# Reordering the LayerNorm and expert loop of a transformer layer on eight cores

## What is computed

```python
x = _layernorm(x + attention(x, wq, wk, wv, wo))      # 16 heads of 128, softmax over 4096 keys
# the expert part, for each row n of x:
logits = x_flat @ Wr.T + br                           # 8 experts
probs = softmax(logits)
expert_idx, expert_weight = argmax(probs), max(probs)
h = einsum('nd,erd->ner', x_flat, A)                  # rank 64 for each expert: 512 columns
y = einsum('ner,eor->neo', h, B) * (1 / 64)
out = y[expert_idx] * expert_weight
x = _layernorm(x + out)
```

## Time and profile before

| | us |
|---|---|
| three timed runs | 4432.73, 4554.11 (the median), 4914.57 |
| profiled execution, device time | 4425.88 |
| its span, slowest core (0) | 4424.3 |
| spans of the eight cores | 4404.7 to 4424.3 |
| mean granted TensorE clock of the cores | 0.880 to 0.884 |

### The profile page before, as it was taken

One profiled execution on the slowest core, in us unless ns is written; L12 is line 12 of the kernel. 1 busy time (PEld: TensorE's weight loads), 2 busy tenths in 40 slices (PEclk: granted clock), 3 DMA queues, 4 the chain that ended last, 5 costly groups with the idle time before them and its releaser, 6 DMA issues.

```text
span 4424.3 us, 52274 instructions; the slowest of 8 cores (4404.7 to 4424.3 us)
## 1 busy us (share of the span) xinstructions
PE 3912.7 (88%) x15488; PEld 1369.4 (31%) x15488; DVE 2271.8 (51%) x4046; ACT 1388.4 (31%) x1574; POOL 187.0 (4%) x303
## 2 busy tenths in 40 slices
PE   6999999999799999999999999999999997835551
PEld 2444444444222222222222222222222233312220
DVE  0000000000388878788878888878887721253443
ACT  1111111111034444444444444444444520201110
POOL 0000000000000000000000000000000000000000
PEclk9999999999778989898989888989998988957776
DMA  9444943393200000000000000000000305120003
GB/s 139 77 76 77 158 77 77 77 146 71 67 1 25 6 20 25 25 1 25 25 25 1 25 25 25 2 24 25 25 1 25 52 6 76 20 38 1 1 1 152
DMA packets 196283, 192.34 MB, mean 43 GB/s; under 512 B 79154, under 2 KB 187826, under 8 KB 192434
## 3 DMA queue, kind: packets, MB, share of 16 engines
q0 software_dynamic: 95408, 88.20, 15.1%
q1 hardware_dynamic: 100610, 100.81, 7.3%
HBM read 218.30 MB, written 58.72 MB: 63 GB/s over the span
## 4 chain that ended last, share of the span: by engine, by line
PE 81%; DVE 8%; issue 5%; DMA 4%; ACT 2%; DVEq 0%; ACTq 0%; POOL 0%; SPq 0%; POOLq 0%
PE psB L524 10%; PE psF L346 10%; PE psA L497 6%; PE psC L497 6%; PE psA L490 6%; PE psC L490 6%; PE psB L199 5%; PE psF L199 5%; PE psC L199 5%; PE psD L642 5%; PE psC L229 3%; PE psB L229 3%; PE psF L229 3%; DVE pa L357 3%; PE psD L752 2%
## 5 line engine op out<-in xcount | busy, mean ns | idle before, releaser
L357 DVE TENSOR_REDUCE pa<-psF 128x1 f32<-128x512 f32 x2048 | 1317.4, 685 | 1504.5 <-PE psF L346 1493.4
L346 PE MATMUL psF<-AB 128*128 128x512 bf16 x2048 | 728.3, 429 | 53.5 <-DVE pa L357 30.8
L474 ACT ACTIVATE AB<-psA 128x1024 bf16<-128x1024 f32 x512 | 523.9, 1023 | 713.8 <-PE psA L497 680.0
L474 ACT ACTIVATE AB<-psC 128x1024 bf16<-128x1024 f32 x512 | 523.9, 1023 | 619.9 <-PE psC L497 590.7
L524 PE MATMUL psB<-AB 128*128 128x512 bf16 x2048 | 621.9, 407 | 0.5 <-ACT AB L474 0.5
L422 DVE TENSOR_TENSOR acc<-acc,AB 128x1024 bf16<-128x1024 bf16 x768 | 525.7, 685 | 43.4 <-ACT AB L474 37.0
L490 PE MATMUL psA<-X,onesmb 1*128 1x512 bf16 x1024 | 343.6, 418 | 33.2 <-ACT obuf L447 30.7
L490 PE MATMUL psC<-X,onesmb 1*128 1x512 bf16 x1024 | 342.5, 417 | 30.3 <-ACT obuf L447 27.9
L346 PEld LDWEIGHTS psF<-AB 128*128 128x128 bf16 x2048 | 216.7, 106 | 443.2 <-issue 287.9
L497 PE MATMUL psC<-AB 128*128 128x512 bf16 x1024 | 346.6, 424 | 0.0
L497 PE MATMUL psA<-AB 128*128 128x512 bf16 x1024 | 346.1, 423 | 0.0
(11 more groups left out here) (81 smaller groups left out, 2202.9 us busy)
## 6 DMA issues: line engine op xcount, KB each, us to landing
C<-xTb POOLq DMA_DIRECT2D x20, 2048.0 KB, 24.3
kdram<-B SPq DMA_DIRECT2D x8, 2048.0 KB, 10.2
vdram<-B SPq DMA_DIRECT2D x32, 512.0 KB, 2.8
AB<-kdram SPq DMA_DIRECT2D x32, 512.0 KB, 3.7
AB<-vdram SPq DMA_DIRECT2D x32, 512.0 KB, 4.5
y<-obuf SPq DMA_DIRECT2D x16, 1024.0 KB, 3.9
AB<-wkT POOLq DMA_DIRECT2D x4, 2048.0 KB, 30.9
AB<-wvT POOLq DMA_DIRECT2D x4, 2048.0 KB, 29.6
```

What stands on the lines that cost most here:

```text
L346: r.op("tensor", lambda eng, ga=ga, qh=qh, par=par, j=j, c=c: eng.matmul(psF[:, (ga % 2) * 512:(ga % 2 + 1) * 512], qbuf(par)[:, qh * 1024 ...
L357: r.op("vector", lambda eng, ga=ga, scc=scc: eng.reduce_max(pa[:, scc:scc + 1], psF[:, (ga % 2) * 512:(ga % 2 + 1) * 512], axis=AX.X), [(S ...
L474: r.op("scalar", lambda eng, gk=gk, slot=slot: eng.activation(ring(gk), slot[:, :], AF.Exp), [(S_["exp"], 1)])
```

## The change

- The 16 sums and squares of the first LayerNorm move into the last column group of the projection, each right behind its tile's residual add. `ln_finalize` takes a range of tiles and is called twice, behind tile 7 and behind tile 15.
- The 16 normalisations stand together ahead of the expert loop, followed by the transposes of tile 0.
- The loop body is cut into functions and emitted in another order: `h` and router of a tile, router chain, mask, then the transposes (and their copies) of the next tile, and after these the transposes of `mh`, `y`, and the statistics of the second LayerNorm.
- The second `ln_finalize` too is called in two halves: behind tile 7 inside the loop, and behind the loop. From tile 8 on each turn of the loop ends with the scaling and the store of tile `qt - 8`; those of tiles 8 to 15 stand behind the loop.
- `Square` writes its squares to `X` (bf16, not used any more at this point) and not to `obuf[1]` (float32).

The bodies of the new functions are the old lines, but for what is shown.

```diff
-    def ln_finalize(r_s1, r_s2, r_a, r_b):
+    def ln_finalize(r_s1, r_s2, r_a, r_b, lo=0, n=16):
         def rng(base):
-            return stcol[:, base:base + 16]
+            return stcol[:, base + lo:base + lo + n]
...
-    r.wait("vector", S_["st1"], 16)
-    r.wait("vector", S_["sq1"], 16)
-    ln_finalize(0, 16, 32, 48)
-    LN1_FIN = S_["vch"].n
+    r.wait("tensor", S_["nrm"], NRM_TOTAL)
+    opidx = 0
+    LN1_FIN1 = LN1_FIN2 = None
+    for g in range(4):
...
+        for qt in range(16):
...
+            opidx += 1
+            if g == 3:
+                r.wait("vector", S_["r1"], 48 + qt + 1)
+                r.op("vector", lambda eng, qt=qt: eng.reduce_sum(
+                    stcol[:, qt:qt + 1], A_[qt][:, :], axis=AX.X), [(S_["st1"], 1)])
+                r.wait("scalar", S_["r1"], 48 + qt + 1)
+                r.wait("scalar", S_["sq1"], S_["sq1"].n)
+                r.op("scalar", lambda eng, qt=qt: eng.activation(
+                    X[:, :], A_[qt][:, :], AF.Square,
+                    accum_out=stcol[:, 16 + qt:17 + qt]), [(S_["sq1"], 1)])
+                if qt == 7:
+                    r.wait("vector", S_["st1"], 8)
+                    r.wait("vector", S_["sq1"], 8)
+                    ln_finalize(0, 16, 32, 48, 0, 8)
+                    LN1_FIN1 = S_["vch"].n
+                if qt == 15:
+                    r.wait("vector", S_["st1"], 16)
+                    r.wait("vector", S_["sq1"], 16)
+                    ln_finalize(0, 16, 32, 48, 8, 8)
+                    LN1_FIN2 = S_["vch"].n
...
-    for qt in range(16):
-        r.wait("vector", S_["vch"], LN1_FIN)
+    def emit_normalize(qt):
+        r.wait("vector", S_["vch"], LN1_FIN1 if qt < 8 else LN1_FIN2)
         r.op("vector", lambda eng, qt=qt: eng.tensor_scalar(
             A_[qt][:, :], A_[qt][:, :], stcol[:, qt:qt + 1], stcol[:, 16 + qt:17 + qt],
...
+    def emit_x1tx(qt):
         r.wait("tensor", S_["n1"], qt + 1)
...
-            tx_i += 1
-
-        r.wait("tensor", S_["txev"], S_["txev"].n)
+    def emit_h_router(qt):
+        hhalf = qt % 2
+        r.wait("tensor", S_["txev"], 16 * (qt + 1))
         if qt == 0:
             r.wait("tensor", S_["wF"], 16)
             r.wait("tensor", S_["bc"], 16)
             r.wait("tensor", S_["ld0g"], 16)
...
+    def emit_router_chain(qt):
+        hhalf = qt % 2
+        lg8 = lgts[:, (qt % 2) * 8:(qt % 2) * 8 + 8]
         r.wait("vector", S_["h"], qt + 1)
...
+    def emit_mask(qt):
+        hhalf = qt % 2
         r.wait("vector", S_["co"], qt + 1)
...
+    def emit_mhtx(qt):
+        hhalf = qt % 2
         r.wait("tensor", S_["mk"], qt + 1)
...
+    def emit_y(qt):
         r.wait("tensor", S_["txes"], S_["txes"].n)
...
+    def emit_ln2_stats(qt):
         r.wait("vector", S_["x2"], 4 * (qt + 1))
         r.op("vector", lambda eng, qt=qt: eng.reduce_sum(stcol[:, 32 + qt:33 + qt],
                                                          A_[qt][:, :], axis=AX.X),
              [(S_["st1"], 1)])
-        r.op("scalar", lambda eng, qt=qt: eng.activation(obuf[1][:, :], A_[qt][:, :],
+        r.op("scalar", lambda eng, qt=qt: eng.activation(X[:, :], A_[qt][:, :],
                                                          AF.Square,
                                                          accum_out=stcol[:, 48 + qt:49 + qt]),
              [(S_["sq1"], 1)])
-    r.wait("vector", S_["st1"], 32)
-    r.wait("vector", S_["sq1"], 32)
-    ln_finalize(32, 48, 0, 16)
-    LN2_FIN = S_["vch"].n
-
-    for qt in range(16):
-        r.wait("vector", S_["vch"], LN2_FIN)
+    def emit_p5(qt, fin):
+        r.wait("vector", S_["vch"], fin)
         r.wait("vector", S_["out"], 16 * (qt - 1))
         r.op("vector", lambda eng, qt=qt: eng.tensor_scalar(
             obuf[qt % 2][:, :], A_[qt][:, :], stcol[:, 32 + qt:33 + qt],
@@ -865,6 +874,33 @@
         r.wait("sync", S_["out"], 16 * qt)
         r.op("sync", lambda eng, qt=qt: eng.dma_start(y.ap()[qt * 128:(qt + 1) * 128, :],
                                                       obuf[qt % 2][:, :]), [(S_["out"], 16)])
+
+    for qt in range(16):
+        emit_normalize(qt)
+    emit_x1tx(0)
+    LN2_FIN1 = None
+    for qt in range(16):
+        emit_h_router(qt)
+        emit_router_chain(qt)
+        emit_mask(qt)
+        if qt + 1 < 16:
+            emit_x1tx(qt + 1)
+        emit_mhtx(qt)
+        emit_y(qt)
+        emit_ln2_stats(qt)
+        if qt == 7:
+            r.wait("vector", S_["st1"], 24)
+            r.wait("vector", S_["sq1"], 24)
+            ln_finalize(32, 48, 0, 16, 0, 8)
+            LN2_FIN1 = S_["vch"].n
+        if qt >= 8:
+            emit_p5(qt - 8, LN2_FIN1)
+    r.wait("vector", S_["st1"], 32)
+    r.wait("vector", S_["sq1"], 32)
+    ln_finalize(32, 48, 0, 16, 8, 8)
+    LN2_FIN2 = S_["vch"].n
+    for qt in range(8, 16):
+        emit_p5(qt, LN2_FIN2)
```

More of the change, by code:

```diff
@@ L628, in build_nc @@
         c_counts[item] = cnt[slot]
[L630 to L635, removed]
-        for qt in range(16):
[L637 to L653, removed]
-    for qt in range(16):
[L656 to L661, removed]
-        r.op("scalar", lambda eng, qt=qt: eng.activation(obuf[1][:, :], A_[qt][:, :],
-                                                         AF.Square,
-                                                         accum_out=stcol[:, 16 + qt:17 + qt]),
-             [(S_["sq1"], 1)])
-    def ln_finalize(r_s1, r_s2, r_a, r_b):
+    def ln_finalize(r_s1, r_s2, r_a, r_b, lo=0, n=16):
         def rng(base):
-            return stcol[:, base:base + 16]
+            return stcol[:, base + lo:base + lo + n]
         r.op("vector", lambda eng: eng.tensor_scalar(rng(r_a), rng(r_s1),
@@ L693, in ln_finalize @@
              [(S_["vch"], 1)])
-    r.wait("vector", S_["st1"], 16)
-    r.wait("vector", S_["sq1"], 16)
-    ln_finalize(0, 16, 32, 48)
-    LN1_FIN = S_["vch"].n
+    r.wait("tensor", S_["nrm"], NRM_TOTAL)
+    opidx = 0
+    LN1_FIN1 = LN1_FIN2 = None
+    for g in range(4):
+        swo = slot_of[("wo", g)]
+        sxr = slot_of[("xr", g)]
+        r.wait("tensor", S_["c" + str(swo)], c_counts[("wo", g)])
+        for qt in range(16):
+            half = opidx % 2
+            r.wait("tensor", S_["r1"], opidx - 1)
+            for dc in range(16):
+                incs = [(S_["op"], 1)] if dc == 15 else []
+                r.op("tensor", lambda eng, g=g, qt=qt, dc=dc, half=half, swo=swo:
+                     eng.matmul(psD[:, half * 512:(half + 1) * 512],
+                                B_[dc // 4][:, (dc % 4) * 2048 + qt * 128:(dc % 4) * 2048 + (qt + 1) * 128],
+                                C_[swo][:, dc * 512:(dc + 1) * 512],
+                                start=(dc == 0), stop=(dc == 15)), incs)
+            r.wait("vector", S_["op"], opidx + 1)
+            if qt == 0:
+                r.wait("vector", S_["c" + str(sxr)], c_counts[("xr", g)])
+            r.op("vector", lambda eng, g=g, qt=qt, half=half, sxr=sxr:
+                 eng.tensor_add(A_[qt][:, g * 512:(g + 1) * 512],
+                                psD[:, half * 512:(half + 1) * 512],
+                                C_[sxr][:, qt * 512:(qt + 1) * 512]), [(S_["r1"], 1)])
+            opidx += 1
[18 more added lines that the diff above has]
+                    LN1_FIN2 = S_["vch"].n
@@ L711, in build_nc @@
     mh_txes_after = {}
-    tx_i = 0
+    tx_state = [0]
     e8_count_at = {}
@@ L723, in build_nc @@
             ALU.mult, ALU.add), [(S_["n1"], 1)])
+    def emit_x1tx(qt):
         r.wait("tensor", S_["n1"], qt + 1)
         for mc in range(16):
-            bank = tx_i % 2
+            bank = tx_state[0] % 2
             if ps_t_last[bank] is not None:
@@ L739, in build_nc @@
             ps_t_last[bank] = (S_["txev"], S_["txev"].n)
-            tx_i += 1
-        r.wait("tensor", S_["txev"], S_["txev"].n)
+            tx_state[0] += 1
+    def emit_h_router(qt):
+        hhalf = qt % 2
+        r.wait("tensor", S_["txev"], 16 * (qt + 1))
         if qt == 0:
@@ L746, in build_nc @@
             r.wait("tensor", S_["ld0g"], 16)
-        hhalf = qt % 2
         r.wait("tensor", S_["mk"], qt - 1)
@@ L765, in build_nc @@
             r.wait("vector", S_["sch"], e8_count_at[qt - 2])
-        lg8 = lgts[:, (qt % 2) * 8:(qt % 2) * 8 + 8]
         r.op("vector", lambda eng, qt=qt, hhalf=hhalf, lg8=lg8:
```

## The result

The changed kernel's median over nine runs is 4472.27 us (4265.31 to 4800.37), that of the kernel before, over ten runs in the same sessions, 4577.56 (4425.88 to 4914.57). Both medians contain executions in which the cores of a die, or of both, are granted a lower clock whatever the kernel; without them (four runs of 4265.31 to 4323.77 are left, and four of 4425.88 to 4432.73 of before) the ratio is 0.9669, with an interval of [0.9593, 0.9745]: 3.3% faster, about 147 us. The direction and the size of the gain are as forecast (4278 / 4425.88 = 0.9666), but the measured time, the median of 4472.27, lies outside the range of 4240 to 4335. Three further executions on record (4264.70, 4577.54 and 4638.96) are not in the median. The profiled execution took 4274.3, with spans of 4239.8 to 4272.8.

What follows compares the result with a forecast made beforehand. The prediction took a serial chain across engines, no single full engine, as the bound. Gains of 17.3 (first `h`), 98.6 (loop) and 32.2 (stores) from 4424.3 gave a span of 4276.2, plus 1.6: 4278 us, range 4240 to 4335.

Steps and rivals of the forecast that it cites:

- The sum: Whole kernel: gains of 17.3 before the loop, 98.6 in it and 32.2 in stores, 148.1 us together, span 4276.2.
- First `h`: Start of the expert loop: first `h` at 3897.1, not 3914.41, released by the load of `BTd`; gain 17.3 us.
- Finalisation behind tile 7: Last column group of the projection: it delays tile 8's add, costing about nothing, at most 3.4 us if cover fails.
- The turn: One tile of the expert loop, from the start of `h`: 20.9 us against 27.85 before.
- The terms inside the loop: Expert loop extras: finalisation behind tile 7 2.65, two `Exp` table loads together 2.6, scalings 1.8 us.
- the 1.8: Expert loop: scalings of tiles 0 to 7 exceed the cover of `h` by 0.26, 7 times, adding 1.8 us.
- The tail: Behind the loop: last sum to first store 7.30 as before, then eight stores in 32.2 us; gain 32.2.
- The clock stays low in `h`: Rival, expert loop: `h` takes 7.5 us and `y` at most 7.2, +75 us, 4353; chance 0.05.
- The clock stays up all through: Rival, expert loop: `y` takes 3.9 us, -1.6 x 16, 4252; chance 0.12.
- The load of `BTd` lands later: Rival, ahead of the loop: the 16 normalisations hold up GpSimd's descriptors, worst case 13 us, 4291; chance 0.04.
- waited for a store: Rival, turns 8 to 15: scalings wait for stores longer than a turn; gain gone at 39 us a store; chance 0.01.

Runs made afterwards that it cites:

- stores alone: Kernel before, old loop order, plus the second finalisation in halves and scaling and store of tile qt-8 in turns 8 to 15: one comparable run, 4411.87 us.
- order alone: Kernel before with only the new loop order, finalisations and stores as before: ratio to before 0.9773, 4323.67 to 4328.77 us.
- the run with two sums: Changed kernel with each tile's sum computed twice in the last column group of the projection: ratio to before 0.9720.
- the last run: Changed kernel with four ScalarE copies a tile, `BTd` awaited at first `y`, residuals of groups 1 to 3 loaded straight into `A_`: ratio to before 0.9352.

## Why the prediction was right in its steps and wrong in its range

- *The range.* This is the step that failed: "The profiled execution (4425.88) lies close to the lowest of the three timed runs (4432.73) and 128 under their median (4554.11); I forecast a run like the profiled one". Two of the three times stood 2.7% and 10.9% above the lowest, and the range of 4240 to 4335 was made from the trace's terms alone, with nothing for that spread. The runs showed the same spread in the changed kernel: four of nine took 4265.31 to 4323.77, around the 4278 of the sum, and five took 4472.27 to 4800.37, so the median fell among these, 137 above the end of the range. Where the same kernel's times scatter by 10%, a range for its median has to contain the scatter, however exact the sum is. The ratio that leaves such runs out came as summed: 0.9669 against 0.9666. Its interval is 0.015 wide, so an agreement to 0.0003 is luck.
- *The sum.* The span was met within 3.4 us, and that too is partly luck: the first `h` came 3.7 later, the loop was 9.3 shorter and the tail 2.2 longer. Each part has the right mechanism; the sizes are off as follows.
- *First `h`.* Right in mechanism and nearly in size: the load is the late one. `BTd` was issued 2.3 later than in the row of before, and landed after 29.4, not 28.1.
- *Finalisation behind tile 7.* Costed at nothing, at most 3.4. TensorE's wait for the delayed add is 0.44. Its three other waits for an add, 13.0 to 13.4 each, stand at the start of column groups, where the add waits for `xnat`, as before (11.4 to 13.0).
- *The turn.* 20.5 for 20.9. `h` 4.18 (4.3), chain and mask 3.5 (3.51), copies to the end of the last 5.8 (5.66). The trace lacks the record of `y`'s first matmul (15 of 16 in the turn shown); put 1.97 ahead of the first add at 3961.48, as before, `y` starts at 3959.5 and takes 5.3 to the next `h` (5.64). About 7 of the 9.3 us are these shorter turns. That the clock would be up in `h` was right, and the run with the transposes moved back shows that it matters.
- *The terms inside the loop.* Finalisation 2.4 (2.65), the `Exp` load in the turn behind it 1.6 (1.28). The scalings come out of their cover as summed: router chain 4.52 behind the start of `h` with a scaling and 4.18 without (4.56 and 4.3). But turns 10 to 15 last 20.4 to 20.6, as those before tile 8: in them the copies take 5.5 (5.5 and 5.9 in turn before), and the four adds of `y` start within 3.3 to 3.5 (3.6 to 3.7). So the 1.8 did not reach the time; why copies and `y` are shorter there is not shown.
- *The tail.* I left out that the scaling of tile 7 stands between the last sum and the second finalisation, 1.25 in the rows above. The first scaling of the last eight starts 6.8 behind the last sum, before 5.9: that makes 1.0 of the 2.2 by which this part was short. The other 1.2 are in the eight stores, 33.4 for 32.2.
- *The rivals.* "The clock stays low in `h`" did not occur, but the run that moves the transposes is close to it: 4321 to 4327, some 50 us above the changed kernel, where the rival put 75. "The clock stays up all through" did not either: the windows over `y` show 0.67 to 0.70. "The load of `BTd` lands later" did not show. In the changed kernel it landed after 29.4 and 28.0 on cores 4 and 5 and after 22.7 to 24.5 on the other six, with 16 normalisations on all of them. Over the six profiled kernels with this block just behind the issue the eight cores have 22.6 to 29.7, over the three in which no normalisation runs beside the load (the one before, stores alone, order alone) 23.1 to 28.1: the ends differ by 1.6 at most, where the rival had 13. Of the rule from the Trainium skill's page "SBUF — State Buffer", section "SBUF: two separate sides", no run here shows the effect. No scaling in the loop waited for a store.

## What to carry to other kernels

Read an in-order queue to its end before you book an overlap: here only two of 16 transposes went ahead, since their copies stood behind the router chain, and batching these copies and moving them to an idle engine took the ratio from 0.9669 to 0.9484. Place dense matmuls behind other dense matmuls: the same `h` took 4.2 there and 6.5 behind sparse transposes. And look at which load is late next before you count a shortened stretch as gained.

## What the runs showed of the hardware

- The load of `BTd` (2 MB), issued 1.1 behind that of `ATd` (2 MB) on the same queue, landed after 22.7 to 29.4 us on the eight cores of one execution, in the execution of before after 23.5 to 28.1. Issued 6.6 behind it (the run with two sums) it took 17.3 to 21.0, and 56 behind it (the last run) 12.5 to 13.9. So about half of its time goes with the load ahead of it.
- A copy of 512 columns of bf16 from `psT` takes about twice as long as one of 128: on VectorE 0.42 against 0.22 (four in a row 1.41), on ScalarE 0.59 against 0.27 (four in a row 2.03). So a column costs about half in the larger copies.
- A shorter turn can run colder. With turns of 20.5 us `y` took 5.3 (granted clock 0.67 to 0.70), with turns of 17.0 it took 6.2 (0.55), with turns of 15 to 16 it took 5.3 and 6.1 in alternate turns (0.72 and 0.57): part of what the shorter chain gained went into the clock.
